# One run of value products per batch for sixteen heads, with four places of probabilities, in a decoder layer

## The chip, the core and the metric

The kernel is written in Bass, one instruction stream per engine, and runs on one core of a Trainium2 chip. The engines are TensorE (PE; its weight loads are listed as PEld), VectorE (DVE), ScalarE (ACT), GpSimd (POOL) and the queue from which SyncE (SP) starts transfers. The metric is the device time of the launch in microseconds. The kernel before took 756.73, 757.1 and 757.51 us in three runs, median 757.1.

## The reference

One decoder layer over 32 batches of 112 tokens and 256 features, in fp32:

```
x = layernorm(x + self_attention(x, W))
x = layernorm(x + cross_attention(x, ctx, mask, Wq, bq, Wk, bk, Wv, bv, Wo, bo))
x = layernorm(x + mixture_of_8_experts_top_2(x, Wr, Wi, Wo))
```

Self-attention takes the softmax of x xT / 16, splits the probabilities at 0.01, divides the large ones by their sum and weighs x with them; the small ones are summed and scale the row sums of W. Cross-attention has 16 heads of 16 features against 375 keys:

```
q, k, v = split_heads(x @ Wq + bq), split_heads(ctx @ Wk + bk), split_heads(ctx @ Wv + bv)
scores = where(mask, -1e15, q @ k.T / 4)
attn = softmax(scores); ctx = attn @ v; return merge_heads(ctx) @ Wo + bo
```

The experts are pairs of matrices (256 x 256) without a nonlinearity between them, so that each pair is multiplied once at the start; a row takes the two experts of largest gate probability.

## The kernel before

**Work of a batch.** For each batch b the PE computes the scores of the 16 heads twice. First by query: `scores(b, n)`, head n, L1444, a tile of 112 queries x 376 keys. The DVE (`head(b, n)`, L975) adds the mask and keeps the row's minimum in `nmax`. `mx0(b)` (L1589) transposes the first eight heads' minima, `mx1(b)` (L1594) the last eight's; ACT (`nmaxT0`, `nmaxT1`) copies them out, and a DMA puts them into the operand of the second product. That one is by key: `score_block(b, i)`, i from 0 to 11, L1462, is a block of 125 keys x 4 heads x 112 queries; four heads are a group, and a group has three blocks. ACT first lays the mask into the block's bank (`lay_mask(b, i)`, L638), PE adds the scores, and ACT takes the exponential into `probsT` (`exponent(b, i)`, L653).

**Value products.** `weigh_values(b, octet)`, L1478, multiplies the probabilities of eight heads with v: 24 matmuls of 17 columns. Four heads stand side by side in the array's four groups of 32 columns (`tile_position=(0, 32 * j)`). Each fp32 matmul is two records in the trace, so a call is 48 records. `weigh_values(b, 0)` waits for exponential 5 of its batch, `weigh_values(b, 1)` for exponential 11. Their results stand in one bank; ACT copies it (`o_sb`, L767), PE transposes it (`oT`, L1600), DVE normalizes it, and `aT`, `Wo` and `y2` follow.

**Probabilities.** `probsT` holds `RING = 3` groups; group g of batch b stands at place (4 b + g) mod 3. So exponential 9, the first of group 3, waits until `weigh_values(b, 0)` is done.

**Order.** Every engine runs its own list of steps, in order, written out by hand for the first three batches and the last five, and as a loop for `it` from 3 to 27. An iteration mixes four batches: scores of `it`, blocks and value products of `it - 1`, the output side of `it - 2`, and projections for `it + 1` and `it + 2`. In it PE goes, in the part that matters here: `m3` (the last expert product of a tile of 128 rows, L1670), block 7, scores 6, block 8, scores 7, `x2T_` (L1514), `PT` (L1495), `weigh_values(it - 1, 0)`, `mx0(it)`, scores 8, block 9, scores 9, `lg` (router, L1651 and L1654), `att` (L1499), block 10, `V2`, scores 10, block 11, `V1`, scores 11, `Sc` (L1488), `weigh_values(it - 1, 1)`, scores 12 and so on. Waits on PE stand at the head of a step: `mx0(it)` waits for the DVE's head 7 of `it`, scores n for head n - 2, block i for its mask on ACT, `lg` for `x2_lo` (DVE, L1143). A tile of rows is missing in every eighth batch, so iterations 11, 19, 27 and 3 have no `m3`, and 10, 18 and 26 no `lg`, `m0`, `m1` and `m2`; these are called short below.

**The other engines around the place.** DVE: head 5, `normalize_x2`, `sparse_den`, the seventh expert sum (`expert(t, 6)`, L1213, which waits for `m3`), head 6, head 7, the eighth expert sum, `sparse_r`, `x2_lo`, and later head 8. ACT: `x2_hi`, mask 9, exponential 8, `sparseT` (L755), `nmaxT0` (L658, waits for `mx0`), mask 10, exponential 9, mask 11, exponential 10, `v2`, exponential 11, ..., mask 0 and mask 1 of the next batch, `o_sb`.

Of the kernel before, what the change touches and what calls it, by code (L numbers as in the profile page):

```python
# [21 lines left out]
ALU = mybir.AluOpType  # L22
# [14 lines left out]
OCTETS = HEADS // 8  # L37
# [3 lines left out]
RING = 3  # L41
# [94 lines left out]
def decoder_layer(nc, x, x_T, context_T, mask, attn_w_T, wq, bq, wk, bk, wv, bv, wo, bo, wr, wi_T, wout,  # L136
                  consts, q_scratch, out):
    ctx = ExitStack()
    with ctx:
# [15 lines left out]
        wo_sb = sb("wo_sb", [128, DC, DIM])  # L155
# [5 lines left out]
        bv_wide = sb("bv_wide", [128, DC, TOK])  # L161
# [19 lines left out]
        vacuum_p = sb("vacuum", [TOK, TOK])  # L181
# [5 lines left out]
        x_casimir = sb("x_cas", [TOK, DIM])  # L187
        sparse_T = sb("sparseT", [TOK, TOK])
        y1_sb = sb("y1", [TOK, DIM])
# [24 lines left out]
        scores_all = sb("scores_left", [128, 2, KEYS])  # L214
        scores_left = scores_all[0:TOK, :, :]
# [9 lines left out]
        y2_sb = sb("y2", [TOK, DIM])  # L225
# [27 lines left out]
        wv_sb = place(scores_all[:, :, :].rearrange("p n k -> p (n k)"), 0)  # L253
# [278 lines left out]
        def _(pool):  # L532
# [95 lines left out]
        def _(act):  # L628
# [14 lines left out]
            def exponent(b, i):  # L643

                place = (GROUPS * b + i // KT) % RING
# [255 lines left out]
        def _(dve):  # L901
# [102 lines left out]
            def vacuum(b):  # L1004
                dve.wait_ge(done["self_p"], b + 1)
                nc.vector.scalar_tensor_tensor(
                    out=vacuum_p[:, :], in0=self_probs[:, :], scalar=THRESH, in1=self_probs[:, :],
# [39 lines left out]
            def stats2(b):  # L1047
                dve.wait_ge(done["y2"], b + 1)
                nc.vector.bn_stats(stats[1][:, :], y2_sb[:, :]).then_inc(done["stats2"], 1)
# [36 lines left out]
            def normalize_x2(b):  # L1086
                dve.wait_ge(done["rstd2"], b + 1)
                nc.vector.tensor_scalar(x2[b % 2][:, :], y2_sb[:, :], moments[1][:, 0:1], rstd[1][:, :],
# [45 lines left out]
            def y2(b):  # L1134
                dve.wait_ge(done["Wo"], b + 1)
                nc.vector.tensor_tensor(y2_sb[:, :], bank_of["Wo"][0:TOK, 0:DIM], x1_plus[b % 3][:, :], ALU.add)\
# [250 lines left out]
        def _(pe):  # L1387
# [80 lines left out]
            def weigh_values(b, octet):  # L1468


                pe.wait_ge(probs_ready, BLOCKS * b + BLOCKS // OCTETS * (octet + 1))
                if b == STACKS - 1 and octet == 0:
                    pe.wait_ge(last_ones, 1)
                for group in (2 * octet, 2 * octet + 1):
                    place = (GROUPS * b + group) % RING
                    for t in range(KT):
                        for j in range(4):
                            mm = nc.tensor.matmul(  # L1478
                                o_bank[32 * j:32 * j + HEAD_DIM + 1, group * TOK:(group + 1) * TOK],
                                v_sb[b % STACKS][0:KP, t, 4 * group + j, :], probsT[:, place, t, j * TOK:(j + 1) * TOK],  # L1480
                                start=(t == 0), stop=(t == KT - 1), tile_position=(0, 32 * j), skip_group_check=True)
                mm.then_inc(pv_done, 1)
# [220 lines left out]
            scores(1, 6); score_block(0, 7); score_block(0, 8); scores(1, 7); weigh_values(0, 0); mx0(1)  # L1703
            scores(1, 8); score_block(0, 9); scores(1, 9); score_block(0, 10); att(3); scores(1, 10); Sc(4)
            score_block(0, 11); V2(1); scores(1, 11); scores(1, 12); weigh_values(0, 1); score_block(1, 0)
# [3 lines left out]
            PT(4); scores(2, 5); score_block(1, 6); score_block(1, 7); weigh_values(1, 0); scores(2, 6)  # L1709
            scores(2, 7); x2T_(0); att(4); score_block(1, 8); scores(2, 8); mx0(2); score_block(1, 9)  # L1710
            scores(2, 9); Sc(5); scores(2, 10); V2(2); scores(2, 11); score_block(1, 10); score_block(1, 11)
            V1(3); scores(2, 12); weigh_values(1, 1); scores(2, 13); V0(3); score_block(2, 0)
# [3 lines left out]
            for it in range(FIRST_WHOLE, LAST_WHOLE + 1):  # L1716
# [14 lines left out]
                at(it - 1, weigh_values, 0)  # L1731
# [17 lines left out]
                at(it - 1, weigh_values, 1)  # L1749
# [41 lines left out]
            score_block(27, 8); score_block(27, 9); PT(30); x2T_(26); weigh_values(27, 0); mx0(28)  # L1791
            scores(28, 8); att(30); score_block(27, 10); lg(22); scores(28, 9); V2(28); score_block(27, 11)
            Sc(31); scores(28, 10); scores(28, 11); weigh_values(27, 1); V0(29); scores(28, 12); oT(27)
# [72 lines left out]
```

## Time and profile before

| what | value |
|---|---|
| runs | 756.73, 757.1, 757.51 us |
| profiled execution, first to last instruction (its span) | 754.8 us |
| around the span, against the median of the runs | 2.3 us |
| PE, PEld, DVE, ACT, POOL busy | 96, 87, 88, 78, 28 % |
| chain that ended last | PE 82 %, DVE 8 %, rest 10 % |
| exponentials (L653) | 384 x 537 ns, 201.9 us |
| heads on DVE (L975) | 512 x 543 ns, 271.1 us |
| value products (L1478) | 3072 records, 86.0 us |

The profile gives the span as the profiled execution's own time; nothing else of that execution's length is listed. Times in rows are microseconds from the span's start. An instruction's duration on PE reaches to its last result and overlaps the next; the distance between two starts says what a matmul costs in a stream.

### The profile page before, as it was taken

How to read it: one execution, taken by the hardware profiler on the slowest of the kernel's cores; microseconds unless marked ns; L12 is line 12 of the kernel's file. 1: busy time of each engine (PE TensorE's matmuls, PEld its weight loads, DVE VectorE, ACT ScalarE, POOL GpSimd, SP SyncE). 2: the span in 40 equal slices, each digit the busy share in tenths (PEclk: the TensorE clock that was granted, in tenths of full speed). 3: DMA queues.
4: the chain of work that ended last, by engine and by line, in shares of the span. 5: the costliest groups of instructions: out<-in, count | busy, mean ns of one | idle time of the engine just before them, and what ended most of it. 6: DMA issues, size and time to landing. Idle time of an engine off the chain costs nothing.

```text
span 754.8 us, 22312 instructions
## 1 busy us (share of the span) xinstructions
PE 727.4 (96%) x7250; PEld 653.9 (87%) x7250; DVE 665.6 (88%) x2608; ACT 589.5 (78%) x1435; POOL 213.1 (28%) x384
## 2 busy tenths in 40 slices
PE   5889999999999999999999999999999999999996
PEld 4769889999989989999899889999999989889874
DVE  4588889999999889999999989999999988998986
ACT  3269988888888898888898898888888898778730
POOL 3242332133333222333321233333213333241001
PEclk8999999999999999999999999999999999999999
DMA  8865664555555465555545566555555556544200
GB/s 259 232 166 145 190 152 128 150 153 151 157 147 146 134 175 151 156 147 151 153 137 144 147 173 160 153 135 161 142 138 155 152 166 165 140 132 138 49 17 27
DMA packets 75668, 110.91 MB, mean 147 GB/s; under 512 B 14224, under 2 KB 59168, under 8 KB 75552
## 3 DMA queue, kind: packets, MB, share of 16 engines
q1 hardware_dynamic: 75552, 109.49, 53.6%
q8 instruction: 58, 0.95, 0.6%
q14 instruction: 58, 0.48, 0.2%
HBM read 50.23 MB, written 18.35 MB: 91 GB/s over the span
## 4 chain that ended last, share of the span: by engine, by line
PE 82%; DVE 8%; issue 3%; DMA 2%; SPq 2%; ACT 1%; POOL 0%; DVEq 0%; POOLq 0%; ACTq 0%
PE psum L1670 19%; PE psum L1444 11%; PE psum L1478 9%; PE psum L1462 9%; PE psum L1537 4%; PE psum L1549 4%; PE psum L1524 4%; PE psum L1619 3%; PE psum L1582 3%; PE psum L1560 2%; PE psum L1571 2%; DVE scores_left L975 2%; DMA k_stack<-k_hi 2%; PE psum L1499 2%; PE psum L1600 2%
## 5 line engine op out<-in xcount | busy, mean ns | idle before, releaser
L975 DVE CUSTOM_DVE_ANT_0 scores_left<-psum,mask_add 112x375 f32<-112x375 f32 x512 | 271.1, 543 | 26.7 <-PE psum L1444 13.8
L653 ACT ACTIVATE probsT<-psum 125x448 f32<-125x448 f32 x384 | 201.9, 537 | 18.9 <-PE psum L1462 15.3
L638 ACT ACTIVATE psum<-mask_u 125x448 f32<-125x448 uint8 x372 | 198.3, 541 | 3.7
L1444 PE MATMUL psum<-k_stack,q_stack 96*112 96x376 f32 x512 | 183.4, 365 | 4.1 <-DMA k_stack<-k_hi 2.0
L1462 PE MATMUL psum<-q_stack,k_stack 97*125 97x224 f32 x768 | 148.7, 280 | 1.8 <-ACT psum L638 1.1
L1462 PEld LDWEIGHTS psum<-q_stack,k_stack 97*125 97x125 f32 x768 | 135.5, 189 | 12.5 <-ACT psum L638 2.3
L1213 DVE SCALAR_TENSOR_TENSOR late<-psum,gate,late 128x256 f32<-128x256 f32 x224 | 107.7, 481 | 12.6 <-PE psum L1670 6.5
L596 POOL TENSOR_TENSOR ctx_lo<-ctx_sb,ctx_hi 128x188 fp32r<-128x188 f32 x128 | 71.3, 588 | 122.8 <-DVE nmax L975 77.7
L1444 PEld LDWEIGHTS psum<-k_stack,q_stack 96*112 96x112 f32 x512 | 89.4, 177 | 15.3 <-issue 6.7
L1670 PE MATMUL psum<-we_hi,x_hi 128*128 128x512 f32 x224 | 91.1, 407 | 0.6 <-DVE gate_nmax L1156 0.6
L1670 PE MATMUL psum<-we_hi,x_lo 128*128 128x512 f32 x224 | 88.5, 395 | 0.0
L1670 PE MATMUL psum<-we_lo,x_hi 128*128 128x512 f32 x224 | 87.8, 392 | 0.0
L1478 PE MATMUL psum<-probsT,v_sb 125*17 125x112 f32 x3072 | 86.0, 260 | 0.2 <-ACT probsT L653 0.2
L1478 PEld LDWEIGHTS psum<-probsT,v_sb 125*17 125x17 f32 x3072 | 69.8, 97 | 9.2 <-ACT probsT L653 1.8
L570 POOL TENSOR_SCALAR var_eps<-moments 128x1 f32<-128x1 f32 x28 | 6.1, 218 | 235.0 <-DVE moments L1079 235.0
L1670 PEld LDWEIGHTS psum<-we_hi,x_lo 128*128 128x128 f32 x224 | 42.0, 188 | 9.9
L559 POOL TENSOR_SCALAR var_eps<-moments 112x1 f32<-112x1 f32 x32 | 6.9, 217 | 147.3 <-DVE moments L1054 147.3
L1670 PEld LDWEIGHTS psum<-we_hi,x_hi 128*128 128x128 f32 x224 | 42.4, 189 | 5.7 <-DVE gate_nmax L1156 0.7
L1670 PEld LDWEIGHTS psum<-we_lo,x_hi 128*128 128x128 f32 x224 | 42.3, 189 | 5.3
L975 DVE DVE_READ_ACCUMULATOR2_ANT nmax<- 112x1 f32 x512 | 42.2, 82 | 0.0
L589 POOL TENSOR_SCALAR mask_add<-mask_u 112x375 f32<-112x375 uint8 x32 | 38.8, 1213 | 8.8 <-DMA mask_u<-in_mask 6.1
L1524 PE MATMUL psum<-x1T,wq_sb 128*128 128x112 f32 x256 | 35.0, 282 | 0.1
(169 smaller groups left out, 1620.9 us busy)
## 6 DMA issues: line engine op xcount, KB each, us to landing
k_stack<-k_hi SPq DMA_DIRECT2D x256, 94.0 KB, 2.5
q_stack<-q_scratch SPq DMA_DIRECT2D x96, 224.0 KB, 3.6
ctx_sb<-in_context_T SPq DMA_DIRECT2D x32, 376.0 KB, 3.7
k_stack<-k_lo SPq DMA_DIRECT2D x128, 94.0 KB, 2.5
q_scratch<-q_hi SPq DMA_DIRECT2D x32, 224.0 KB, 2.1
q_scratch<-q_lo SPq DMA_DIRECT2D x32, 224.0 KB, 2.0
xT<-in_x_T SPq DMA_DIRECT2D x32, 112.0 KB, 2.4
x_sb<-in_x SPq DMA_DIRECT2D x32, 112.0 KB, 3.0
```

The costliest lines, as they stand in the source:

```text
L589: nc.gpsimd.tensor_scalar(mask_add[b % 2][:, :], mask_u8[b % MASKS][0:TOK, 0:KEYS], BIG, None, ALU.mult)\
L596: part = nc.gpsimd.tensor_tensor(ctx_lo[b % 2][:, c, keys], ctx_sb[b % 2][:, c, keys], ctx_hi[b % 2][:, c, keys].bitcast(fp32), ALU.subtract)
L638: nc.scalar.activation(psum[0:KP, ST_BANKS[i % 2], 0:4 * TOK].rearrange("p (h q) -> p h q", h=4), mask_u8[b % MASKS][:, KEYS + t * TOK:KEY ...
L653: nc.scalar.activation(probsT[:, place, i % KT, :], psum[0:KP, ST_BANKS[i % 2], 0:4 * TOK], ACT.Exp, scale=-1.0).then_inc(probs_ready, 1)
L975: nc.vector.tensor_tensor_reduce(scores_left[:, n % 2, :], psum[0:TOK, S_BANKS[n % 2], 0:KEYS], mask_add[b % 2][:, :], 1.0, 3.0e38, ALU.ad ...
L1213: nc.vector.scalar_tensor_tensor(out=mix[:, :], in0=mix_bank(t, f"m{e // 2}")[0:ROWS, (e % 2) * DIM:(e % 2 + 1) * DIM], scalar=gates[t % 2 ...
L1444: nc.tensor.matmul(psum[0:TOK, S_BANKS[n % 2], 0:KEYS_EVEN], q_stack[s][0:96, pair, odd, c, :], k_stack[s][0:96, pair, c, :], start=True, ...
L1462: mm = nc.tensor.matmul(psum[0:KP, ST_BANKS[i % 2], 2 * e * TOK:2 * (e + 1) * TOK].rearrange("p (h q) -> p h q", h=2), k_stack[s][:, pair, ...
L1478: mm = nc.tensor.matmul(o_bank[32 * j:32 * j + HEAD_DIM + 1, group * TOK:(group + 1) * TOK], v_sb[b % STACKS][0:KP, t, 4 * group + j, :], ...
L1524: mm = nc.tensor.matmul(bank_of["qT"][:, r * TOK:(r + 1) * TOK], wq_sb[:, c, r * 128:(r + 1) * 128], x1T[:, c, :], start=(c == 0), stop=(c ...
L1537: mm = nc.tensor.matmul(bank_of["K0"][:, 0:KEYS_EVEN], w_part[:, c, 0 * 128:1 * 128], x_part[:, c, :], start=(n == 0), stop=(n == 3 * DC - 1))
L1670: mm = nc.tensor.matmul(mix_bank(t, name)[0:ROWS, 0:width], x_part[:, c, :], w_part[:, c, :], start=(n == 0), stop=(n == len(parts) - 1))
```

## The change

The two value product steps of a batch become one, at the place of the second, for groups 0 to 3 in turn; each group has its own wait (for its third exponential) and its own increment of `pv_done`. Only the last batch keeps two steps, groups 0 and 1 and then 2 and 3. `probsT` gets four places, one for each group, so an exponential that starts a group waits for the same group's products of the batch before. To make room in SBUF, some tiles share memory: `y2` is written over `x1_bo`, `x_cas` into `y1`, the small probabilities over `self_exp`, and the raw Wv, Wo and the wide bv lie in `probsT` during the setup. These bring three waits: the first exponential waits for the splitting of Wo and for the bias product, and POOL's `x1_bo(b)` waits for `x2` of batch b - 3.

```diff
-RING = 3
+RING = GROUPS
...
             def x1_bo(b):
...
+                if b >= 3:
+                    pool.wait_ge(done["x2"], b - 2)
                 nc.gpsimd.tensor_tensor(x1_plus[b % 3][:, :], x1[b % 2][:, :], bo_row[:, :], ALU.add)
...
             def exponent(b, i):
-                place = (GROUPS * b + i // KT) % RING
+                place = i // KT
...
-                overwritten = GROUPS * b + i // KT - RING
-                if i % KT == 0 and overwritten >= 0:
-                    act.wait_ge(pv_done, overwritten // 2 + 1)
+                if b == 0 and i == 0:
+                    act.wait_ge(split_done, 7)
+                    act.wait_ge(setup_pe, 3)
+                if i % KT == 0 and b > 0:
+                    act.wait_ge(pv_done, GROUPS * (b - 1) + i // KT + 1)
...
             def o_sb(b):
-                act.wait_ge(pv_done, OCTETS * (b + 1))
+                act.wait_ge(pv_done, GROUPS * (b + 1))
...
-            def weigh_values(b, octet):
-                pe.wait_ge(probs_ready, BLOCKS * b + BLOCKS // OCTETS * (octet + 1))
-                if b == STACKS - 1 and octet == 0:
+            def weigh_values(b, *groups):
+                if b == STACKS - 1 and groups[0] == 0:
                     pe.wait_ge(last_ones, 1)
-                for group in (2 * octet, 2 * octet + 1):
-                    place = (GROUPS * b + group) % RING
+                for group in groups:
+                    pe.wait_ge(probs_ready, BLOCKS * b + KT * (group + 1))
...
-                mm.then_inc(pv_done, 1)
+                    mm.then_inc(pv_done, 1)
...
                 at(it + 2, PT)
-                at(it - 1, weigh_values, 0)
                 at(it, mx0)
...
-                at(it - 1, weigh_values, 1)
+                at(it - 1, weigh_values, 0, 1, 2, 3)
                 at(it, scores, 12)
```

The lists of DVE, ACT, POOL and SP keep their order; only PE's changes. The first place is around `mx0` in an iteration. On PE, before (block 8, scores 7, `x2T_`, `PT`, value products, `mx0`, scores 8, block 9):

```order
L1462 MATMUL psum<-q_stack,k_stack 125x224 x2
L1444 MATMUL psum<-k_stack,q_stack 112x376
L1514 MATMUL psum<-const_sb,x_0 128x112 x2
L1495 MATMUL psum<-const_sb,sparse 112x112
L1478 MATMUL psum<-probsT,v_sb 17x112 x24
L1589 MATMUL psum<-const_sb,nmax 8x112
L1444 MATMUL psum<-k_stack,q_stack 112x376
L1462 MATMUL psum<-q_stack,k_stack 125x224 x2
```

On PE at the same place, now (lines are 2 to 4 lower in the changed file):

```order
L1460 MATMUL psum<-q_stack,k_stack 125x224 x2
L1442 MATMUL psum<-k_stack,q_stack 112x376
L1510 MATMUL psum<-const_sb,x_0 128x112 x2
L1491 MATMUL psum<-const_sb,sparse 112x112
L1585 MATMUL psum<-const_sb,nmax 8x112
L1442 MATMUL psum<-k_stack,q_stack 112x376
L1460 MATMUL psum<-q_stack,k_stack 125x224 x2
```

The 24 value products between `PT` and `mx0` are gone, and `mx0` follows `PT` directly.

The second place is between scores 11 and scores 12. On PE, before (scores 11, `Sc`, value products, scores 12, block 0):

```order
L1444 MATMUL psum<-k_stack,q_stack 112x376
L1488 MATMUL psum<-xT 112x112 x2
L1478 MATMUL psum<-probsT,v_sb 17x112 x24
L1444 MATMUL psum<-k_stack,q_stack 112x376
L1462 MATMUL psum<-q_stack,k_stack 125x224 x2
```

On PE at the second place, now:

```order
L1442 MATMUL psum<-k_stack,q_stack 112x376
L1484 MATMUL psum<-xT 112x112 x2
L1474 MATMUL psum<-probsT,v_sb 17x112 x48
L1442 MATMUL psum<-k_stack,q_stack 112x376
L1460 MATMUL psum<-q_stack,k_stack 125x224 x2
```

Here the run has grown from 24 to 48 matmuls.

## Rows read from the trace of the kernel before

**Rows 1.** The page's first line and its busy times.

```profile
span 754.8 us, 22312 instructions
...
PE 727.4 (96%) x7250; PEld 653.9 (87%) x7250; DVE 665.6 (88%) x2608; ACT 589.5 (78%) x1435; POOL 213.1 (28%) x384
```

**Rows 2.** Busy time in stretches: length, each engine (instructions), granted clock, DMA.

```profile
256.43:275.06 18.63, 17.58 (x201) 15.51 (x200) 16.21 (x67) 17.40 (x43) 6.47 (x12) 1.00 0.62 166
297.23:319.38 22.15, 22.15 (x229) 20.33 (x228) 20.66 (x84) 18.57 (x45) 6.51 (x12) 1.00 0.52 144
...
660.00:755.00 95.00, 85.69 (x832) 73.50 (x830) 79.89 (x285) 53.74 (x131) 16.19 (x33) 0.98 0.26 72
```

**Rows 3.** Waits: engine, tile, line <- releaser: us in total, times, longest.

```profile
DVE late L1213 <- PE psum L1670: 6.5, 24, 0.3
...
ACT nmaxT L658 <- PE psum L1589: 5.0, 21, 1.7
```

**Rows 4.** PE in order of time: start us, duration us, engine, line, tiles, count.

```profile
295.84 0.40 PE L1670 MATMUL psum<-we_hi,x_lo 128*128 128x512 f32 x1
...
296.85 0.36 PE L1514 MATMUL psum<-const_sb,x 112*128 112x112 f32 x2
297.04 0.26 PE L1495 MATMUL psum<-const_sb,sparse 112*112 112x112 f32 x1
297.23 1.34 PE L1478 MATMUL psum<-probsT,v_sb 125*17 125x112 f32 x48
298.50 0.26 PE L1589 MATMUL psum<-const_sb,nmax 112*8 112x112 f32 x1
...
299.17 0.18 PE L1651 MATMUL psum<-wr_parts,x_hi 128*128 128x16 f32 x1
...
299.85 0.57 PE L1462 MATMUL psum<-q_stack,k_stack 97*125 97x224 f32 x2
...
302.73 0.48 PE L1478 MATMUL psum<-probsT,v_sb 125*17 125x112 f32 x12
...
304.00 0.43 PE L1444 MATMUL psum<-k_stack,q_stack 96*112 96x376 f32 x1
```

**Rows 5.** DVE in order of time, same stretch.

```profile
296.27 0.48 DVE L1213 SCALAR_TENSOR_TENSOR late<-psum,gate,late 128x256 f32<-128x256 f32 x1 [0.30 <-PE psum L1670]
296.81 0.55 DVE L975 CUSTOM_DVE_ANT_0 scores_left<-psum,mask_add 112x375 f32<-112x375 f32 x1
...
297.28 0.55 DVE L975 CUSTOM_DVE_ANT_0 scores_left<-psum,mask_add 112x375 f32<-112x375 f32 x1
297.75 0.08 DVE L975 DVE_READ_ACCUMULATOR2_ANT nmax<- 112x1 f32 x1
...
298.22 0.38 DVE L1143 TENSOR_TENSOR x_lo<-psum,x_hi 128x224 fp32r<-128x224 f32 x1
```

**Rows 6.** ACT in order of time, same stretch.

```profile
298.39 0.26 ACT L755 ACTIVATE sparseT<-psum 112x112 f32<-112x112 f32 x1
298.80 0.25 ACT L658 ACTIVATE nmaxT<-psum 8x112 fp32r<-8x112 f32 x1 [0.15 <-PE psum L1589]
298.96 0.52 ACT L638 ACTIVATE psum<-mask_u 125x448 f32<-125x448 uint8 x1
```

**Rows 7.** DVE and weight load, batch 2's first transpose of maxima.

```profile
81.92 0.08 DVE L975 DVE_READ_ACCUMULATOR2_ANT nmax<- 112x1 f32 x1
...
82.06 0.08 PEld L1589 LDWEIGHTS psum<-const_sb,nmax 112*8 112x8 f32 x1 [0.29 <-DVE nmax L975]
```

**Rows 8.** ACT and PE in two short iterations, 10 and 11.

```profile
258.16 0.52 ACT L638 ACTIVATE psum<-mask_u 125x448 f32<-125x448 uint8 x1
...
258.73 0.29 PEld L1462 LDWEIGHTS psum<-q_stack,k_stack 97*125 97x125 f32 x2 [0.19 <-ACT psum L638]
...
276.82 0.52 ACT L638 ACTIVATE psum<-mask_u 125x448 f32<-125x448 uint8 x1
...
277.67 0.57 PE L1462 MATMUL psum<-q_stack,k_stack 97*125 97x224 f32 x2
```

**Rows 9.** PE, ACT, POOL and DVE at the places of the three new waits.

```profile
23.69 1.02 PE L1412 MATMUL psum<-wo_sb,bv_wide 128*112 128x256 f32 x4
...
49.03 0.54 ACT L653 ACTIVATE probsT<-psum 125x448 f32<-125x448 f32 x1
...
79.29 0.74 POOL L582 TENSOR_TENSOR x_bo<-x,bo_row 112x256 f32<-112x256 f32 x1
86.08 1.19 POOL L589 TENSOR_SCALAR mask_add<-mask_u 112x375 f32<-112x375 uint8 x1 [6.05 <-DMA mask_u<-in_mask]
...
80.11 0.40 DVE L1088 TENSOR_SCALAR x<-y,moments,rstd 112x256 f32<-112x256 f32 x1
```

More of the change, by code:

```diff
@@ L252, in decoder_layer @@
         wk_sb = place(probsT_all, 6)
-        wv_sb = place(scores_all[:, :, :].rearrange("p n k -> p (n k)"), 0)
+        wv_sb, wo_sb, bv_wide = place(probsT_all, 7), place(probsT_all, 8), place(probsT_all, 9)[:, :, 0:TOK]
         v_last = v_sb[STACKS - 1][:, :, :, :].rearrange("p t h d -> p (t h d)")
@@ L1006, in vacuum @@
                 nc.vector.scalar_tensor_tensor(
-                    out=vacuum_p[:, :], in0=self_probs[:, :], scalar=THRESH, in1=self_probs[:, :],
+                    out=self_exp[:, :], in0=self_probs[:, :], scalar=THRESH, in1=self_probs[:, :],
                     op0=ALU.is_lt, op1=ALU.mult, accum_out=vac_sum[:, :]).then_inc(done["vacuum"], 1)
@@ L1048, in stats2 @@
                 dve.wait_ge(done["y2"], b + 1)
-                nc.vector.bn_stats(stats[1][:, :], y2_sb[:, :]).then_inc(done["stats2"], 1)
+                nc.vector.bn_stats(stats[1][:, :], x1_plus[b % 3][:, :]).then_inc(done["stats2"], 1)
             def mom2(b):
@@ L1479, in weigh_values @@
                                 o_bank[32 * j:32 * j + HEAD_DIM + 1, group * TOK:(group + 1) * TOK],
-                                v_sb[b % STACKS][0:KP, t, 4 * group + j, :], probsT[:, place, t, j * TOK:(j + 1) * TOK],
+                                v_sb[b % STACKS][0:KP, t, 4 * group + j, :], probsT[:, group, t, j * TOK:(j + 1) * TOK],
                                 start=(t == 0), stop=(t == KT - 1), tile_position=(0, 32 * j), skip_group_check=True)
-                mm.then_inc(pv_done, 1)
+                    mm.then_inc(pv_done, 1)
             def Sc(b):
@@ L1702, in _ @@
             scores(1, 3); K0(2); PT(3); scores(1, 4); score_block(0, 6); scores(1, 5); expert_product(6)
-            scores(1, 6); score_block(0, 7); score_block(0, 8); scores(1, 7); weigh_values(0, 0); mx0(1)
+            scores(1, 6); score_block(0, 7); score_block(0, 8); scores(1, 7);  mx0(1)
             scores(1, 8); score_block(0, 9); scores(1, 9); score_block(0, 10); att(3); scores(1, 10); Sc(4)
-            score_block(0, 11); V2(1); scores(1, 11); scores(1, 12); weigh_values(0, 1); score_block(1, 0)
+            score_block(0, 11); V2(1); scores(1, 11); scores(1, 12); weigh_values(0, 0, 1, 2, 3); score_block(1, 0)
             scores(1, 13); score_block(1, 1); V0(2); oT(0); V1(2); score_block(1, 2); scores(1, 14)
@@ L1790, in _ @@
             scores(28, 4); score_block(27, 7); qT(29); scores(28, 5); scores(28, 6); m3(21); scores(28, 7)
-            score_block(27, 8); score_block(27, 9); PT(30); x2T_(26); weigh_values(27, 0); mx0(28)
+            score_block(27, 8); score_block(27, 9); PT(30); x2T_(26);  mx0(28)
             scores(28, 8); att(30); score_block(27, 10); lg(22); scores(28, 9); V2(28); score_block(27, 11)
-            Sc(31); scores(28, 10); scores(28, 11); weigh_values(27, 1); V0(29); scores(28, 12); oT(27)
+            Sc(31); scores(28, 10); scores(28, 11); weigh_values(27, 0, 1, 2, 3); V0(29); scores(28, 12); oT(27)
             scores(28, 13); score_block(28, 0); score_block(28, 1); V1(29); aT(27); m0(22); scores(28, 14)
@@ L1798, in _ @@
             score_block(28, 7); scores(29, 6); m3(22); PT(31); scores(29, 7); scores(29, 8)
-            score_block(28, 8); x2T_(27); weigh_values(28, 0); mx0(29); score_block(28, 9); scores(29, 9)
+            score_block(28, 8); x2T_(27);  mx0(29); score_block(28, 9); scores(29, 9)
             score_block(28, 10); att(31); scores(29, 10); V2(29); score_block(28, 11); lg(23); scores(29, 11)
-            scores(29, 12); weigh_values(28, 1); scores(29, 13); V1(30); scores(29, 14); V0(30); oT(28)
+            scores(29, 12); weigh_values(28, 0, 1, 2, 3); scores(29, 13); V1(30); scores(29, 14); V0(30); oT(28)
             scores(29, 15); m0(23); score_block(29, 0); score_block(29, 1); aT(28); mx1(29); m1(23); Wo(28)
@@ L1805, in _ @@
             scores(30, 4); qT(31); score_block(29, 6); scores(30, 5); scores(30, 6); m3(23)
[L1806 removed]
+            score_block(29, 7); scores(30, 7); score_block(29, 8); x2T_(28);  lg(24)
             mx0(30); scores(30, 8); scores(30, 9); score_block(29, 9); score_block(29, 10); V2(30)
             scores(30, 10); m0(24); scores(30, 11); score_block(29, 11); scores(30, 12); V0(31)
[L1809 removed]
+            weigh_values(29, 0, 1, 2, 3); scores(30, 13); scores(30, 14); V1(31); oT(29); score_block(30, 0)
             score_block(30, 1); scores(30, 15); m1(24); aT(29); score_block(30, 2); mx1(30)
```

30 lines of the change are left out of this document (11 added, 19 removed).

## The prediction, made before the changed kernel was run

> **What bounds the kernel now.** I read the busy times first, then the same by stretches, then the list of waits, and then one iteration in order of time on PE, DVE and ACT. The reader is to see one thing in each.
>
> The busy times [rows 1] put PE first, at 727.4 of 754.8 us, and DVE second. By stretches [rows 2] an ordinary iteration (12, from 297.23 to 319.38) has PE busy for 22.15 of its 22.15 us. A short one, without a tile of rows, has PE at 17.58 of 18.63 and ACT at 17.40, and the end (660 to 755) has PE at 85.69 of 95. A busy PE need not be a full one, so the order of time has to decide: in an ordinary iteration PE's steps follow each other at the distances that streams of the same kind have elsewhere, and no wait of PE in it is in the list. So what shortens PE's row of work shortens the kernel, and what makes PE wait lengthens it.
>
> The list of waits [rows 3] shows who lives close to PE. The DVE's expert sum waits for the last expert product 24 times, 6.5 us in all, 0.27 each: the DVE is there before PE. ACT waits for `mx0` 21 times, 0.24 each in the mean. Both stand right around the step that is moved.
>
> **What is removed.** The first value product run starts 0.19 after `PT` and `mx0` starts 1.27 after the run [rows 4]: 1.46 from `PT` to `mx0`. Without the run `mx0` would follow at the distance of two fp32 transposes: the pair of `x2T_` takes 0.36 with 0.26 for the last, so 0.10. PE is therefore 1.36 us earlier at `mx0`, if nothing holds it.
>
> **What is added.** 48 records in a run of 1.34 us and 12 in 0.48 [rows 4] give (1.34 - 0.48) / 36 = 0.024 a record, 0.096 for four records that stand side by side. 24 more matmuls are 48 records: 48 x 0.024 = 1.15 us at the second place. The rest of the removed 1.36, 0.21 us, is the entry and the exit of a run: 0.19 in place of about 0.10 before it, and 0.19 after its last record in place of a stream's step. That is the gain per batch which the change can have, at 31 merged batches 31 x 0.21 = 6.5 us.
>
> The Trainium skill, "TensorEngine Tiling (Array Packing)", Key Properties, has this as a rule: changing the tiling mode drains the array, changing the tile does not. The rows on entry and exit agree; by that rule alone the sum would be the 6.5 us just worked out, and it is the first rival below.
>
> **What the removed run covered.** `mx0` waits for the DVE's head 7. In iteration 12 [rows 5] the chain is: the last expert product starts at 295.84 and lasts 0.40 [rows 4], the DVE's sum follows at 296.27 (it had waited 0.30), head 6 at 296.81, head 7 at 297.28, and its minimum is written at 297.75 + 0.08 = 297.83. That chain begins at a PE step which stands before the change's place and keeps its distance to it, so it does not move. The shortest distance from such a write to the dependent PE step is 0.06 us: 82.00 to 82.06 where PE did wait [rows 7]. So `mx0` can start at 297.89 at the earliest. Before it stood at 298.50, after the value products. Instead of 1.36 us PE comes out 0.61 us early and stands idle for 0.75. PE takes its steps in order, so scores 8 and all that follows are held with it.
>
> Next in line, the same iteration:
> - `lg` at 299.17 needs `x2_lo`, 298.22 + 0.38 = 298.60, plus 0.06: it can be 0.51 early. That DVE step follows head 7 and is not earlier than before.
> - Block 10 at 299.85 needs mask 10 on ACT. It ends at 298.96 + 0.52 = 299.48 [rows 6], and 0.05 is the wait's distance in the one case where PE waited for it (258.68 to 258.73 [rows 8]): 0.32 early if ACT stays. But ACT was idle for 0.15 before `nmaxT0`, which waits for `mx0`, so it moves by 0.15 with it: 0.47 early. 0.15 is what the row calls idle; ACT's steps overlap by some 0.08, so up to the 0.51 of `lg` is possible. I take 0.48.
> - Heads 8 and 9, `sparseT`, `V2`, `V1`, block 11 and `Sc` have more room than that before them; of the DVE's steps there, head 8 is the nearest to a step of PE.
>
> So the long run starts 0.48 early and is 1.15 longer: scores 12 comes 1.15 - 0.48 = **0.67 us later** in an ordinary iteration. Everything behind it (scores 12, `oT`, `aT`, `Wo`, the expert products) moves with it, and the next iteration has the same wait again, since its chain starts from its own expert product. Nothing pays it back: PE had no idle time to use up. The bounds: 0.61 early (only `mx0` holds) costs 0.54, 0.32 early (ACT does not move) costs 0.83, nothing early costs 1.15.
>
> **The other costs of the edit**, each at nothing, with its cover:
> - Four waits and four increments in a run in place of one and one per half: the exponentials of groups 0 to 2 are long done; exponential 11 is now needed only before the run's last quarter, three quarters (1.7 us) after its start. Bounds 0 to 0.06 a boundary.
> - `exponent` of a group waits for the same group a batch before. That run stands ahead of the next batch's block 0 on PE, and exponential 0 needs that block, so the wait is always over. A fourth place frees exponential 9; it comes behind mask 10 (298.96 [rows 6]), when the first run had ended (297.23 + 1.34 = 298.57 [rows 4]), so nothing is won there.
> - `o_sb` on ACT now stands behind a run that ends 0.67 later; self-exponential and exponential 0 are queued behind it, and PE needs them for steps that are 0.67 later too. Before, `o_sb` had little spare time, so this is where ACT stays tied to PE in short iterations.
> - The new waits [rows 9]: the bias product ended at 24.7 and exponential 0 started at 49.03. `x1_bo(3)` started at 79.29 and now waits for an `x2` that ends at 80.51, 1.2 us later; behind it on POOL is a mask step that itself waited for a transfer until 86.08. All later ones have microseconds to spare.
> - Shared tiles: DVE runs in order and the steps keep their order. Nothing.
>
> **The sum.** Whole iterations, 3 to 27, are 25. Ordinary in this place are 18, and iteration 3 (no `m3`, but ACT and `lg` as in ordinary ones): 19 x 0.67 = 12.7 us. In 10, 18 and 26 PE already waited for mask 10, 0.19 on its weight load [rows 8]; only the 0.15 of ACT can be won: 1.00 each, 3.0 us. In 11, 19 and 27 mask 10 ends at 277.34 and block 10 starts at 277.67, ACT without idle time before it: 0.28 early, 0.87 each, 2.6 us. Together 18.3 us. The other six merged batches lie in the written-out beginning and end; there PE waits for the DVE already at several heads, so little is early (near 1.0 each, 6 in all), but PE's 9.3 us of idle time in the end [rows 2] can swallow a part. I take 4, between 0 and 6.9 (6 x 1.15). Span: 754.8 + 18.3 + 4 = 777.1 us. The profiled execution's span is 2.3 under the median 757.1, so the time is 777.1 + 2.3 = **779.4 us**.
>
> **The rivals.**
> 1. The gain is real: `mx0` does not wait, since head 7 comes sooner or the 0.67 is overestimated throughout. Then 31 x 0.21: 757.1 - 6.5 = 750.6 us. For it speaks that 0.21 is measured on every run. Against it: head 7's write at 297.83 is 0.69 after the place where `mx0` would stand (297.14), in an iteration whose neighbours look the same. It decides where head 7 is written less than 0.1 after `PT` starts. 5%.
> 2. ACT does not come earlier, so block 10 holds PE to 0.32: 19 x 0.83 + 3 x 1.15 + 2.6 + 5 = 26.9, 784 us. For it: mask 10 also hangs on exponential 8, and ACT is at 18.57 of 22.15. Against: the 0.15 of idle time before `nmaxT0`. 12%.
> 3. No step is early at all, and the long run also makes the DVE wait for scores 12 without a later gain: 31 x 1.15 = 35.7, 792.8 us. The DVE's 20.66 of 22.15 speaks a little for it. 4%.
> 4. PE has room that its busy time hides, and the 0.67 vanishes in it: 757 us, no change. Against it are the distances between PE's steps, which are those of a full stream. 3%. The Trainium skill, "Perfetto Trace Analysis", Identifying the Most-Contended Engine, calls matmul busy time a bad measure of how near the PE is to its roofline and takes the weight loads' share instead. By that share, 20.33 of 22.15 [rows 2], 1.8 us of an iteration would be spare and this case the likely one; the distances in the order of time do not bear it out here.
>
> The forecast itself has 76%: 779.4, with its own range from 771 (0.54 in 25 iterations, 13.5, and nothing at the edges: 770.6) to 784. Slower by over 0.2% (about what a measurement of this kernel can tell from no change) is cases 2, 3 and the forecast: 92%. Faster is 5%, within it 3%. The range of 8 in 10 goes from 771 to 786: it takes in case 2 and leaves out 1, 3 and 4.
>
> **What the profile after would show.** PE idle, or its weight load, before L1585 in nearly every iteration, 0.6 to 0.8 us, put down to the DVE's head; a short wait before `lg` or block 10; ordinary iterations of 22.8 us in place of 22.15; runs of 96 records of 2.5 us; ACT's idle time before `o_sb` up by half a microsecond; DVE work per iteration unchanged, its share lower. It would be wrong if `mx0` follows `PT` at 0.1, if iterations shrink to 21.9, or if the wait is there but scores 12 is not late.

## The result, and the profile after

The changed kernel took 789.7 us, median of four runs (786.44 to 796.47), the kernel before 757.03 beside it. The ratio is 1.0432, interval [1.0401, 1.0462]: 32.7 us slower, where 22.3 were forecast (779.4 us) and 786 was the upper end. The direction was right, the size was not.

The page of after, its first line and its busy times:

```profile
span 787.9 us, 22312 instructions
...
PE 731.5 (93%) x7250; PEld 662.1 (84%) x7250; DVE 666.9 (85%) x2608; ACT 590.7 (75%) x1435; POOL 213.6 (27%) x384
```

The span is 33.1 longer than in [rows 1], PE's idle time 29 us more (56.4 in place of 27.4). PE's busy time is up by 4.1 although its work is the same; that becomes plain below.

The list of waits of after, columns as in [rows 3]:

```profile
DVE scores_left L973 <- PE psum L1442: 47.0, 62, 1.8
ACT o_sb L765 <- PE psum L1474: 36.0, 32, 2.6
...
PEld psum L1585 <- DVE nmax L973: 34.4, 30, 1.5
PE psum L1585 <- DVE late L1211: 23.8, 22, 1.4
...
DVE late L1211 <- PE psum L1666: 5.9, 23, 0.3
```

`mx0` (L1585, the first transpose of maxima) now waits in nearly every iteration, some 1.1 us each time. Two rows name two releasers for the same step: its weight load waited for the DVE's head, the matmul for the DVE's expert sum (L1211). The forecast knew the first alone. The last row answers to [rows 3]: the DVE still waits for the last expert product, since its chain hangs on PE and has not moved. ACT and DVE now wait for PE at the other end, ACT's `o_sb` for the long run (36.0 us in all; before it was 2.5, so some 1.0 us more a batch, where the forecast had half a microsecond), the DVE for the scores behind it.

PE of after in order of time, iteration 12, which answers to [rows 4]:

```profile
305.64 0.33 PE L1442 MATMUL psum<-k_stack,q_stack 96*112 96x376 f32 x1
305.81 0.38 PE L1460 MATMUL psum<-q_stack,k_stack 97*125 97x224 f32 x2
...
306.20 0.35 PE L1510 MATMUL psum<-const_sb,x 112*128 112x112 f32 x2
306.40 0.26 PE L1491 MATMUL psum<-const_sb,sparse 112*112 112x112 f32 x1
307.73 0.26 PE L1585 MATMUL psum<-const_sb,nmax 112*8 112x112 f32 x1 [1.08 <-DVE late L1211]
...
308.38 0.17 PE L1647 MATMUL psum<-wr_parts,x_hi 128*128 128x16 f32 x1
...
311.94 2.49 PE L1474 MATMUL psum<-probsT,v_sb 125*17 125x112 f32 x96
314.37 0.43 PE L1442 MATMUL psum<-k_stack,q_stack 96*112 96x376 f32 x1
```

`PT` to `mx0` is 1.33 us, though nothing stands between them; with the run it was 1.46. So `mx0` is 0.13 earlier, not 0.61. This is its lead: the time by which it could have started sooner, had PE been there. The run itself is as forecast: 2.43 us from its start to scores 12, before 1.27 (302.73 to 304.00), so 1.16 more.

The DVE of after, same stretch, and behind it the one DVE row of the kernel before that stood in the gap of [rows 5]:

```profile
307.11 0.08 DVE L973 DVE_READ_ACCUMULATOR2_ANT nmax<- 112x1 f32 x1
307.11 0.48 DVE L1211 SCALAR_TENSOR_TENSOR late<-psum,gate,late 128x256 f32<-128x256 f32 x1
...
307.57 0.37 DVE L1141 TENSOR_TENSOR x_lo<-psum,x_hi 128x224 fp32r<-128x224 f32 x1
```

```profile
297.75 0.48 DVE L1213 SCALAR_TENSOR_TENSOR late<-psum,gate,late 128x256 f32<-128x256 f32 x1
```

Head 7's minimum is written at 307.11 + 0.08 = 307.19, yet `mx0` starts 0.54 after it and 0.14 after the end of the eighth expert sum (307.11 + 0.48 = 307.59). In the code this is `free("mx0", b)`: `mx0` writes G2, one of three PSUM banks that the small products share in turn. The user of G2 ahead of it is `m3`, and `m3`'s result is read last by that sum. The row of before gives 297.75 + 0.48 + 0.14 = 298.37, and `mx0` stood at 298.50: the lead was 0.13 all along.

All of the loop shows this. In the 21 iterations with an `m3`, `mx0` of after starts 0.15 behind the sum's end each time; before it was 0.27 or 0.28 in 20 of them and 0.15 in one. In the four without an `m3` (3, 11, 19, 27) the sum has no part in it: there `mx0` of after starts 0.06 behind head 7's write, where before it was 0.77 or 0.78. With head 7 as the only releaser the lead was 0.71.

By stretches, which answers to [rows 2]: iteration 12; a short one; the iteration from 240.65; 3.41 us of that one.

```profile
307.73:330.87 23.14, 22.06 (x228) 20.42 (x229) 20.68 (x84) 18.68 (x46) 6.49 (x12) 1.00 0.53 138
265.38:284.11 18.73, 17.58 (x200) 15.48 (x201) 15.60 (x63) 16.72 (x43) 6.49 (x12) 1.00 0.56 152
240.65:265.38 24.73, 23.65 (x228) 21.85 (x228) 21.14 (x84) 18.75 (x46) 6.49 (x12) 0.93 0.50 135
241.87:245.28 3.41, 3.41 (x15) 3.21 (x15) 2.59 (x12) 1.87 (x5) 0.79 (x2) 0.50 0.33 109
```

An ordinary iteration is 23.14 us, not 22.8; the short one is only 0.10 longer than in [rows 2], for what it loses shows in the iteration behind it (the two together 42.35 in place of 40.80). The fourth row is a second thing that the forecast lacked: for 3.41 us the granted clock is 0.50, the 1.2 GHz level. After has five such stretches between 62 and 751 us, at 241.9, 378.4, 426.2, 651.5 and 743.6; before has none there. (Both have one in the first 25 us and one at the very end; before has a further one at 55.3, with PE busy for nearly all of it, that after lacks, so some of the clock's loss in before lies in its beginning.) The iteration around the first of them is 24.73 us long (third row). PE in order of time there:

```profile
240.65 0.26 PE L1585 MATMUL psum<-const_sb,nmax 112*8 112x112 f32 x1 [1.08 <-DVE late L1211]
...
241.67 0.99 PE L1495 MATMUL psum<-x_sb,sparseT 112*112 112x256 f32 x2
242.09 0.96 PE L1460 MATMUL psum<-q_stack,k_stack 97*125 97x224 f32 x2
...
248.87 0.43 PE L1442 MATMUL psum<-k_stack,q_stack 96*112 96x376 f32 x1
```

From `mx0` to scores 12 it is 8.22 us here and 6.64 in iteration 12: one stretch costs 1.58 us. The clock falls 1.2 us after `mx0`, so behind the idle time and not in it; the other four fall 1.2, 1.2, 1.6 and 2.3 us after an `mx0`. PE counts as busy meanwhile: 23.65 us in this iteration, 22.06 in iteration 12. That is where its busy time grew.

`mx0` of iterations 3 and 28, in after and in before, gives the sum over the loop:

```profile
101.66 0.26 PE L1585 MATMUL psum<-const_sb,nmax 112*8 112x112 f32 x1 [0.48 <-DVE nmax L973]
...
674.91 0.26 PE L1585 MATMUL psum<-const_sb,nmax 112*8 112x112 f32 x1 [0.74 <-DVE nmax L973]
```

```profile
101.94 0.26 PE L1589 MATMUL psum<-const_sb,nmax 112*8 112x112 f32 x1
...
646.77 0.26 PE L1589 MATMUL psum<-const_sb,nmax 112*8 112x112 f32 x1
```

573.25 against 544.83, 28.4 us more. Four of the five stretches lie in it, 4 x 1.58 = 6.3; 22.1 is left for lateness. The ends (all that lies outside the loop) hold 33.1 - 28.4 = 4.7.

### The profile page after: what moved, and what is told of

It is laid out like the page before. It is cut to its first block, busy times and chain, and to the rows that moved or that the text cites. A ratio compares the mean times of both kernels' runs of the same rounds, so it can differ in the third digit from the quotient of the medians.

```text
span 787.9 us, 22312 instructions
## 1 busy us (share of the span) xinstructions
PE 731.5 (93%) x7250; PEld 662.1 (84%) x7250; DVE 666.9 (85%) x2608; ACT 590.7 (75%) x1435; POOL 213.6 (27%) x384
## 4 chain that ended last, share of the span: by engine, by line
PE 81%; DVE 10%; issue 5%; ACT 3%; DMA 1%; SPq 1%; POOL 1%; DVEq 0%; POOLq 0%; ACTq 0%
PE psum L1666 18%; PE psum L1442 10%; PE psum L1474 9%; PE psum L1460 9%; PE psum L1533 4%; PE psum L1545 4%; DVE late L1211 3%; PE psum L1578 3%; PE psum L1520 3%; PE psum L1556 3%; PE psum L1615 3%; PE psum L1567 3%; DVE scores_left L973 2%; PE psum L1495 2%; PE psum L1596 2%
## 5 line engine op out<-in xcount | busy, mean ns | idle before, releaser
L1460 PE MATMUL psum<-q_stack,k_stack 97*125 97x224 f32 x768 | 151.5, 284 | 2.2 <-ACT psum L634 1.5
L1211 DVE SCALAR_TENSOR_TENSOR late<-psum,gate,late 128x256 f32<-128x256 f32 x224 | 107.8, 481 | 11.1 <-PE psum L1666 5.9
L1474 PE MATMUL psum<-probsT,v_sb 125*17 125x112 f32 x3072 | 80.5, 260 | 0.0
L1474 PEld LDWEIGHTS psum<-probsT,v_sb 125*17 125x17 f32 x3072 | 72.0, 98 | 4.4 <-ACT probsT L651 0.7
L765 ACT ACTIVATE o_sb<-psum 128x448 f32<-128x448 f32 x32 | 17.4, 545 | 36.0 <-PE psum L1474 36.0
```

Source lines behind the costliest of these rows:

```text
L1211: nc.vector.scalar_tensor_tensor(out=mix[:, :], in0=mix_bank(t, f"m{e // 2}")[0:ROWS, (e % 2) * DIM:(e % 2 + 1) * DIM], scalar=gates[t % 2 ...
L1460: mm = nc.tensor.matmul(psum[0:KP, ST_BANKS[i % 2], 2 * e * TOK:2 * (e + 1) * TOK].rearrange("p (h q) -> p h q", h=2), k_stack[s][:, pair, ...
L1474: mm = nc.tensor.matmul(o_bank[32 * j:32 * j + HEAD_DIM + 1, group * TOK:(group + 1) * TOK], v_sb[b % STACKS][0:KP, t, 4 * group + j, :], ...
```

## The experiments

Two theories stood after this. **Bank**: `mx0` is held by the expert sum through the bank that it shares with `m3`; without that it would be 0.61 early, as forecast. **Clock**: the idle time at `mx0` makes the clock fall now and then, and each fall costs time beside the lateness. Rivals were a price of the new waits and shared tiles, and a price of the long run itself.

| kernel | expected us | us | ratio to before, interval | loop over before | half-clock stretches in the loop |
|---|---|---|---|---|---|
| the change | 779.4, 771 to 786 | 789.7 | 1.0432 [1.0401, 1.0462] | 28.4 | 4 of 3.4 |
| the change, again | 785 to 796 | 790.83 | 1.0433 [1.0393, 1.0474] | 28.5 | 4 of 3.4 |
| own bank | 776 to 782 | 782.45 | 1.0346 [1.0316, 1.0376] | 20.4 | 1 of 6.8 |
| fill, four products | 780 to 783 | 783.59 | 1.0345 [1.0315, 1.0376] | 22.0 | none |
| own bank and three products | 775 to 778 | 778.62 | 1.0264 [1.0244, 1.0283] | 17.2 | none |
| late `mx0` | 4.5 under the change | 787.33 | 1.0376 [1.0329, 1.0423] | 26.0 | 2 of 6.8 |
| two runs, ends merged | 760 to 762 | 762.72 | 1.0076 [1.0051, 1.01] | 0.2 | none |
| two runs, four places kept | 757, ratio 0.998 to 1.002 | 755.51 | 0.9971 [0.9946, 0.9996] | 3.4 | 1 of 6.8 |
| the same, again | ratio 0.997 to 0.999 | 757.72 | 1.0002 [0.9973, 1.003] | 0.4 | none |
| run split by scores 12 | 762.3 | 765.15 | 1.0107 [1.008, 1.0134] | 7.5 | none |
| early value projection | 755 to 759 | 767.34 | 1.0109 [1.0059, 1.016] | 9.1 | none |

"Loop over before" is the distance between `mx0` of iterations 3 and 28, less 544.83, from one profiled execution each; a stretch of 6.8 us costs it some 3 us (3.2 with own bank, below; 3.4 - 0.4 = 3.0 with two runs, whose profiled execution, at 764.54 us, was the longest of its ten). The kernel before, run beside the experiments, took 757.81 to 757.84 us. Six experiments came out 0.5 to 2.9 us above what was expected of them, the early value projection 8.3.

**Two runs, with everything else of the change kept.** In the loop, the beginning and the end alike:

```diff
+                at(it - 1, weigh_values, 0, 1)
                 at(it, mx0)
...
-                at(it - 1, weigh_values, 0, 1, 2, 3)
+                at(it - 1, weigh_values, 2, 3)
```

> The changed kernel with its four places of probabilities, its shared tiles and its new waits, but with the two value product runs of a batch back at their old places. Theory (all of the loss comes from the order on PE): 757 us, ratio 0.998 to 1.002. Rival (the shared memory or the waits for a batch before cost something): 760 us or more.

755.51 us, and measured again:

> The four places of probabilities with two runs at their old places, once more with more rounds. Theory (an exponential that starts group 3 no longer follows a run, iterations were 22.12 us in place of 22.15 on the profile): ratio 0.997 to 0.999, a gain of 1 to 2 us. Rival (the earlier ratio of 0.997 came from the clock of single runs): 1.000 within its interval.

757.72, ratio 1.0002 [0.9973, 1.003]. The small gain of the first measurement did not come again. So the four places, the waits by group, the new waits and the shared tiles cost nothing that can be measured (at most 2.3 us, by the interval), and the 32.7 us belong to where the value products stand.

**Only the ends merged.** The loop as in the diff above; batches outside it keep one run.

> The changed kernel with two runs per batch in the 25 whole iterations and one run only for the six batches of the written-out beginning and end. Theory (from the two traces: the 25 whole iterations carry 28.4 of the 33.1 us, clock included): 3 to 5 us above the kernel before, 760 to 762 us, ratio 1.004 to 1.007. Rival (the loss at the ends is given back, since PE has idle time there): 757 us.

762.72, so 4.9 us over the 757.83 beside it (3.9 to 7.6 by the interval), with the loop at 0.2. That is the term of the ends by itself, and the loop's part of the change is the rest.

**`mx0` in a bank of its own.** It writes the value products' bank and waits until that bank's content of two batches ago has been read:

```diff
+        bank_of["mx0"] = psum[:, O_BANK, :]
...
             def weigh_values(b, *groups):
+                if b < BATCH - 1 and groups[0] == 0:
+                    pe.wait_ge(done["nmaxT0"], b + 2)
...
             def mx0(b):
                 pe.wait_ge(max_ready, HEADS * b + 8)
-                free("mx0", b)
+                if b >= 2:
+                    pe.wait_ge(done["o_norm"], b - 1)
```

> The changed kernel, but the first transpose of maxima writes into the bank of the value products, which is free at that place, so it no longer waits for the eighth expert sum (its old bank was last used by the last expert product). The merged run then waits for ACT's copy of the maxima. Theory (that bank wait holds PE): the distance from PT to mx0 falls from 1.34 to about 0.8, iterations from 23.14 to about 22.8, time 776 to 782 us, fewer stretches at the 1.2 GHz level. Rival (head 7 alone holds PE, the other wait is a name only): no change, 787 to 796 us.

782.45. PE and DVE of this kernel in order of time, iteration 13:

```profile
328.47 0.26 PE L1494 MATMUL psum<-const_sb,sparse 112*112 112x112 f32 x1
329.32 0.26 PE L1589 MATMUL psum<-const_sb,nmax 112*8 112x112 f32 x1 [0.59 <-DVE nmax L974]
...
330.07 0.28 PE L1651 MATMUL psum<-wr_parts,x_hi 128*128 128x16 f32 x1
...
336.16 0.42 PE L1443 MATMUL psum<-k_stack,q_stack 96*112 96x376 f32 x1
```

```profile
329.18 0.08 DVE L974 DVE_READ_ACCUMULATOR2_ANT nmax<- 112x1 f32 x1
...
329.64 0.37 DVE L1142 TENSOR_TENSOR x_lo<-psum,x_hi 128x224 fp32r<-128x224 f32 x1
```

and its list of waits:

```profile
PEld psum L1589 <- DVE nmax L974: 24.3, 30, 1.3
...
PEld psum L1651 <- DVE x_lo L1142: 4.3, 19, 1.3
```

Now `PT` to `mx0` is 0.85, 0.61 less than before, and head 7's write is 0.06 ahead of it: the forecast's two figures. `lg` is the next to wait, 19 times, as forecast; its first matmul starts 0.06 after `x2_lo` ends (329.64 + 0.37). The expert sum has gone from the list as a releaser. By stretches, the iteration, then one with a half-clock stretch:

```profile
329.32:352.18 22.86, 22.27 (x228) 20.39 (x229) 20.59 (x84) 18.54 (x46) 6.57 (x12) 1.00 0.53 145
280.20:306.46 26.26, 25.44 (x227) 23.22 (x227) 19.83 (x81) 19.06 (x47) 5.69 (x10) 0.87 0.49 132
281.51:288.34 6.83, 6.83 (x43) 6.38 (x46) 3.29 (x16) 5.09 (x13) 1.19 (x3) 0.50 0.49 139
```

Iterations are 22.86 where the forecast said 22.8; the time is 0.45 above its range, with one long half-clock stretch in the loop. The bank theory holds: the rival's 787 is excluded. The last row is a stretch twice as long; it makes that iteration 26.26, 3.2 more than the same one of the kernel with own bank and three products (23.08). Without it the loop is 17.2 over before (20.4 - 3.2).

**Idle products ahead of `mx0`.** Four products of 512 columns that nothing reads, so that PE is busy while it would wait:

```diff
+            def fill(b):
+                if b >= 2:
+                    pe.wait_ge(done["o_norm"], b - 1)
+                for _ in range(4):
+                    nc.tensor.matmul(o_bank[:, 0:DIM * 2], we_hi[:, 0, 0:128], we_hi[:, 0, 0:DIM * 2],
+                                     start=True, stop=True, skip_group_check=True)
...
+                at(it, fill)
                 at(it, mx0)
```

> The changed kernel with four idle products of 512 columns between PT and mx0 in the 25 whole iterations: they compute nothing that is used, and run while PE would stand idle for 1.2 us. Theory (five stretches at the 1.2 GHz level came from that idle time and cost 1.6 us each): none in the loop, iterations stay at 23.14, time 780 to 783 us. Rival (the level falls for another reason, or the products delay mx0): 787 us or more.

783.59. PE in order of time and the stretch of an iteration:

```profile
327.88 0.26 PE L1491 MATMUL psum<-const_sb,sparse 112*112 112x112 f32 x1
327.91 1.17 PE L1587 MATMUL psum<-we_hi 128*128 128x512 f32 x4
329.22 0.26 PE L1593 MATMUL psum<-const_sb,nmax 112*8 112x112 f32 x1
```

```profile
329.22:352.37 23.15, 23.01 (x232) 21.05 (x233) 20.68 (x84) 18.66 (x46) 6.47 (x12) 1.00 0.56 153
```

`PT` to `mx0` is still 1.34 and the iteration 23.15: the products fit into the hole and delay nothing. (Only in the four iterations without an `m3` is the hole too short for them: `mx0` starts 0.34 behind head 7's write there, not 0.06. Iterations 10 and 11 together take 42.33, no more than in after.) What is gone is every half-clock stretch of the loop, and the loop is 22.0 over before in place of 28.4; 6.3 was worked out above. The clock theory holds: 6 us of the result are the clock, and the idle time at `mx0` is what lets it fall there.

The profiles are single ones, but the other executions say the same. The mean granted clock was 0.975 to 0.987 in the eight of the change, 0.983 to 0.988 in the four of own bank, and 0.991 to 0.996 in the four with four idle products, which ran on the same chip as own bank. The change itself was not run on that chip; the ratios of the two, each to the kernel before beside it, have intervals that do not meet (1.0315 to 1.0376, and 1.0401 to 1.0462). In the kernel before it was 0.984 to 0.997 beside these experiments, so that one loses some clock now and then too; no profile places these losses.

**Both together**, with three products, since the hole is shorter:

> The changed kernel with the first transpose of maxima in the free bank and three idle products of 512 columns ahead of it in the 25 whole iterations (they compute nothing that is used). Theory (two causes, the bank wait and the clock, that add up): iterations stay at 22.86 us, no stretch at 1.2 GHz in the loop, 775 to 778 us, 6 us under the kernel with the idle products alone and 2 to 7 under the one with the free bank alone. Rival (the two are one cause): no faster than the better of the two, 782 us.

778.62, below either alone (the intervals do not meet), 5.0 and 3.8 us less where 6 and 2 to 7 were expected. The stretch of the iteration that answers to the two above:

```profile
328.36:351.22 22.86, 22.86 (x231) 20.84 (x231) 20.59 (x84) 18.51 (x46) 6.50 (x12) 1.00 0.54 145
```

The loop is 17.2 over before, where the forecast had 18.3. With both unforeseen causes taken away the kernel comes near what was forecast for the change: 20.8 us over the 757.81 beside it, where 22.3 had been forecast. It is not quite the forecast's kernel: two more stretches lie in its beginning (42.3 and 56.0 us) and one in its end.

**The change once more**, beside the next kernels:

> The changed kernel once more, unchanged, on the chip of the three others: 785 to 796 us, as far apart as the number of stretches at the 1.2 GHz level in each run.

790.83. Five stretches again, three of them in the same iterations (240.8, 425.2, 650.4) and two elsewhere (285.2, 722.1), each beginning 1.1 to 2.1 us after an `mx0`, and the loop is 28.5 over before.

**Late `mx0`.** Scores 8, block 9 and scores 9 move ahead of it:

```diff
-                at(it, mx0)
                 at(it, scores, 8)
                 at(it - 1, score_block, 9)
                 at(it, scores, 9)
+                at(it, mx0)
                 at_tile(it - 2, lg)
```

> The changed kernel with scores 8, block 9 and scores 9 moved ahead of mx0 in the 25 whole iterations; nothing else. Theory (PE waits at whichever step stands first behind a late producer; the expert sum's end holds mx0, head 6 holds scores 8, mask 9 holds block 9): PE stands idle in three short pieces, mask 10 on ACT (behind the copy of the maxima) then caps the lead at about 0.34 us, iterations of 22.96 us in place of 23.14, about 4.5 us less than the changed kernel. Rival (the place of mx0 makes no difference, the lead is lost anyway): 23.14 and no change.

787.33. PE in order of time (scores 8, block 9),

```profile
327.12 0.42 PE L1442 MATMUL psum<-k_stack,q_stack 96*112 96x376 f32 x1
327.78 0.48 PE L1460 MATMUL psum<-q_stack,k_stack 97*125 97x224 f32 x2 [0.24 <-ACT psum L634]
```

the weight load of block 10 in the same iteration,

```profile
329.31 0.29 PEld L1460 LDWEIGHTS psum<-q_stack,k_stack 97*125 97x125 f32 x2 [0.25 <-ACT psum L634]
```

and the stretch of an iteration:

```profile
328.28:351.24 22.96, 22.60 (x229) 20.32 (x227) 20.62 (x85) 18.45 (x46) 6.50 (x12) 1.00 0.55 144
```

With `mx0` out of the way PE waits for head 6 (scores 8), then for mask 9 and for mask 10 on ACT, and the iteration is only 0.18 shorter, the 22.96 that was expected. Mask 10 stands on ACT behind the copy of the maxima, so that moving `mx0` back delays it; block 10 starts 0.05 behind its end in 22 of the 25 iterations. So there is no single wait to take away here: heads, masks and the sum stand one behind the other, each some tenths from holding PE. The clock falls here too, though the idle time of PE is in pieces. The time is 3.5 us under the change's 790.83 on the same chip, but the two intervals overlap; the gain is seen in the iterations alone.

**Real work into the hole.** `V0` of the next batch moves from behind scores 13 to behind `PT` and writes the value products' bank, the order of the last experiment is kept, and the beginning and the end have two runs.

```diff
                 at(it + 2, PT)
+                at(it + 1, V0)
                 at(it, scores, 8)
                 at(it - 1, score_block, 9)
                 at(it, scores, 9)
+                at(it, mx0)
...
-                at(it, nmaxT0)
                 before_last(it - 1, lay_mask, 10)
+                at(it, nmaxT0)
                 at(it - 1, exponent, 9)
+                at(it + 1, v0)
```

> The merged run in the 25 whole iterations, but its old first place is filled with work: V0 of the next batch (0.71 us), which writes into the free bank of the value products, then scores 8, block 9, scores 9 and only then mx0; on ACT mask 10 comes ahead of the copy of the maxima, and the copy of V0 follows exponential 9. The ends keep two runs per batch. Theory (a merged run costs 1.15 us less the lead; the lead is about 0.5 and V0 takes 0.71 out of the part behind): iterations of 22.1 us as before, 755 to 759 us, no extra stretch at 1.2 GHz. Rival (the loss is in the merged run itself, or ACT's added copy becomes the bound): 765 us or more.

767.34, where the change with its ends undone would take some 785 by an estimate (789.7 - 4.7). The iteration, and the waits of this kernel:

```profile
326.89:349.38 22.49, 22.49 (x229) 20.30 (x227) 20.30 (x85) 18.23 (x47) 6.51 (x12) 1.00 0.55 147
```

```profile
PEld psum L1473 <- ACT psum L645: 7.1, 31, 0.5
...
PEld psum L1614 <- ACT o_sb L776: 5.4, 26, 0.9
```

22.49 in place of 23.14: real work gets 0.65 back, not the 1.0 that was expected. The time lies in the rival's range. PE now waits for masks (31 times) and `oT` for `o_sb` (26 times), about 0.2 us each; both stand on ACT, as the rival's second half has it. Which part of the missing 0.35 is theirs was not tested. The merged loop stays 0.35 longer than the one with two runs.

**What a pair of entry and exit costs.** In the kernel before, the second run is cut in two by scores 12:

```diff
-                at(it - 1, weigh_values, 1)
+                at(it - 1, weigh_values, 1, 0)
                 at(it, scores, 12)
+                at(it - 1, weigh_values, 1, 1)
```

> The kernel before with scores 12 moved into the middle of the second value product run in the 25 whole iterations, so one entry and one exit of a run more per iteration, with the same matmuls. Theory (an entry and an exit cost 0.21 us together): 25 x 0.21 = 5.3 us more, 762.3 us, ratio 1.007. Rival (the merged run gained nothing by its missing entry and exit, they overlap other work): 757 us, ratio 1.000.

765.15, 7.3 us more, 7.5 in the loop. PE in order of time:

```profile
325.95 0.77 PE L1478 MATMUL psum<-probsT,v_sb 125*17 125x112 f32 x24
326.65 0.43 PE L1444 MATMUL psum<-k_stack,q_stack 96*112 96x376 f32 x1
327.01 0.77 PE L1478 MATMUL psum<-probsT,v_sb 125*17 125x112 f32 x24
327.71 0.48 PE L1462 MATMUL psum<-q_stack,k_stack 97*125 97x224 f32 x2
```

Scores 12 takes 0.36 to the next run, where a step of scores takes 0.17 in a stream (305.64 to 305.81 in after). The two half runs take 1.40 and the whole one 1.27. So a pair costs 0.32 us between scores, not 0.21: the price depends on the neighbours. It is real and of the size of the gain that the change was to bring; the rival here, that it hides behind other work, is excluded. Whether the first rival's 6.5 us could have been had is not shown, since each merged kernel measured here has waits of PE that cost more.

## Why the prediction was right and wrong

**Right**: PE's row of work bounds the kernel, and the removed run covered a lead. PE stands idle at `mx0` in each iteration, the added records come through whole at the second place (1.16 for 1.15), and nothing pays them back. The edits costed at nothing cost nothing: 1.0002 [0.9973, 1.003]. The ends were put at 4, and measured 4.9 alone (3.9 to 7.6) and 4.7 in the change's profile, each profile with one half-clock stretch in its end; so near an agreement is partly luck, since no term of the clock stood in the 4. The DVE's time of an iteration is 20.68, before 20.66; the run is 2.49 long, as said.

**Wrong, first**: the step "`mx0` can start at 297.89 at the earliest". It took head 7 as the only releaser. `mx0` also waits for the eighth expert sum, which stands behind head 7 on the DVE, through the bank that `m3` wrote. The row lay between two that were read [rows 5], and the condition is in the code (`free`, and `m3` as the user of G2 ahead of `mx0`). With it the working gives 0.13 early in place of 0.61, and 1.15 - 0.13 = 1.02 for the 0.67; the iterations show 0.99 (23.14 - 22.15). Over the loop this is 4.8 us: 22.0 with idle products, 17.2 with them and the bank of its own. The steps after it (`lg` 0.51, block 10 0.48) held in that kernel within 0.1: scores 12 is 0.71 late there. The list of waits could not show the second releaser, since `mx0` did not wait for the sum anywhere before the change, and for head 7 only outside the loop.

**Wrong, second**: no term for the clock. The sum took idle time of PE to cost its length alone. Four stretches in the loop and one in the end, 5 x 1.58 = 7.9 us, are the larger part of the miss, and all but 1.6 of it lies in the loop. Products that compute nothing took the loop's 6.3 away. The first mistake by itself would have left the time inside the range (779.4 + 3.8 = 783.2, by the account that follows); it was the clock that took it out.

The miss of 10.3 us adds up: lateness in the loop 22.1 in place of 18.3 (4.8 for the bank, less 1.1 by which the rest cost less than forecast), 3.8; the clock in the loop 6.3; the ends 4.7 in place of 4, 0.7; around the span 1.8 in place of 2.3, -0.5. The 1.1 has a likely source, which was not tested: in the loop before, six ordinary iterations were 0.2 to 0.5 us longer than 22.15, and in after one was so much longer than 23.14. So the difference of two typical iterations counts some of them too dear.

The rivals: the gain without a wait did not occur, nor did PE's hidden room, for 1.15 us of added records made the run 1.16 longer and each iteration 0.99. The case of 784 (ACT holds PE) comes nearer the number than the forecast, but not by what happened: block 10 waited for its mask only in short iterations. The case of 792.8 (nothing early) was nearer than the forecast at this place, where 0.13 was measured, but for a reason that the profile does not bear out: its DVE load.

**Open**: why the clock falls after some of these idle times and not after others of the same length, why a stretch is sometimes twice as long, and why one fell in the loop of a kernel without them (two runs, at 618.7 us). Where the longer iterations of the loop before come from was not looked into.

## What to carry to other kernels

Before a step of PE is said to be free to move, list all its conditions from the code. One of them is the reader of the former content of its output bank. Find each one's end in the order of time: a list of waits names only the one that came last, and none while the step is late for another reason. A run of work that is taken from ahead of a step with conditions is worth its length only up to the nearest lead, and on a PE without idle time what is added elsewhere comes through whole. Where a change leaves PE idle over and over, price the clock as well, and test it by putting products without a reader into the hole.

## What the runs showed of the hardware beyond that

Short idle times of PE that come back in each iteration went with a loss of clock. With 1.1 us of idle time at `mx0` the loop had four stretches of 3.4 us at the 1.2 GHz level in each of two profiled executions, at 1.58 us each; with 0.6 us (own bank) it had one of 6.8 us; with PE kept busy there it had none, in one profiled execution each of two kernels. Four products of 512 columns put into a hole of 1.1 us delayed nothing.

The price of going into a run of side-by-side tiles and out of it was 0.21 us next to transposes (1.36 - 1.15, before), and 0.36 - 0.17 + 0.13 = 0.32 between scores of 376 columns.
